# Attention with the value products in groups of four key steps, and the exponentials in a ring of eight

## The reference

```python
qkv = jnp.einsum('bsd,od->bso', x, w_project)          # x is layer-normed, 1 x 2048 x 512
q, k, v = (qkv[0], qkv[1], qkv[2])                     # 16 heads of 32
att = jnp.einsum('bhqd,bhkd->bhqk', q, k) / math.sqrt(HEAD_DIM)
att = jnp.where(causal[None, None, :, :], jnp.float32(-1000000000.0), att)
att = jax.nn.softmax(att, axis=-1)
out = jnp.einsum('bhqk,bhkd->bhqd', att, v)
return jnp.einsum('bsd,od->bso', out, w_out)           # and x + this
```

## Time and profile before

| | |
|---|---|
| median of 3 runs | 3358.98 us (3356.23 to 3374.25) |
| profiled execution: its own time is its span | 3356.4 us |
| TensorE matmuls, busy share of the span | 93% |
| DVE / ACT / POOL | 62% / 47% / 26% |
| attention, pairs 1 to 7 and the tail | about 291 to 820 us of the span |

### The profile page before, as it was taken

One profiled execution on the slowest core, in us unless ns is written; L12 is line 12 of the kernel. 1 busy time (PEld: TensorE's weight loads), 2 busy tenths in 40 slices (PEclk: granted clock), 3 DMA queues, 4 the chain that ended last, 5 costly groups with the idle time before them and its releaser, 6 DMA issues. The chain is left out here.

```text
span 3356.4 us, 62801 instructions
## 1 busy us (share of the span) xinstructions
PE 3138.2 (93%) x15964; PEld 2447.5 (73%) x15965; DVE 2074.8 (62%) x3588; ACT 1589.8 (47%) x2095; POOL 885.0 (26%) x768
## 2 busy tenths in 40 slices
PE   7979999999899899999999968878998999999996
PEld 6745555555577699999999933336777999999995
DVE  4256666663585466666666649988654666666664
ACT  2224444444321256665665656634124665565663
POOL 0011000010011233334343314430122444343432
PEclk9969999999999999999999979989998999999998
DMA  5331111130310367777777540124016777777765
GB/s 175 114 76 40 40 40 39 40 99 4 114 37 23 110 174 167 174 175 167 182 180 173 109 131 0 50 72 159 21 42 173 180 174 178 175 172 175 168 139 111
DMA packets 141339, 383.49 MB, mean 114 GB/s; under 512 B 22112, under 2 KB 22880, under 8 KB 137568
## 3 DMA queue, kind: packets, MB, share of 16 engines
q1 hardware_dynamic: 87456, 252.66, 24.1%
q0 software_dynamic: 52608, 127.69, 20.1%
q10 hardware_dynamic: 1152, 1.57, 0.2%
HBM read 281.42 MB, written 104.63 MB: 115 GB/s over the span
## 5 line engine op out<-in xcount | busy, mean ns | idle before, releaser
L1727 DVE TENSOR_TENSOR first_lo<-first_raw,first_hi x232 | 562.8, 2426 | 118.9 <-ACT first_hi L1670 118.4
L1624 POOL DMA_INDIRECT acc_rows<-g_y,first_ids_out x232 | 377.6, 1628 | 896.3 <-ACT g_y L1681 698.3
L594 DVE TENSOR_REDUCE b_part_max<-b_p_ring 128x1 f32<-128x512 f32 (+3 forms) x640 | 360.1, 606 | 230.9 <-PE b_p_ring L681 143.4
L1670 ACT ACTIVATE first_hi<-first_raw x232 | 469.5, 2024 | 49.9 <-DMA first_raw<-in_expert_weights_dram 30.9
L568 ACT ACTIVATE b_probs<-b_p_cols 128x1024 f32<-128x1024 f32 (+1 forms) x320 | 269.2, 893 | 322.5 <-PE b_p_cols L699 322.5
L1720 DVE TENSOR_TENSOR g_hidden<-g_gate,g_p_up 128x352 f32<-128x352 f32 x232 | 120.9, 521 | 449.2 <-PE g_p_up L1787 444.8
L1785 PE MATMUL g_p_gate<-first_hi,g_rows_hi 128*128 x928 | 321.6, 347 | 6.7 <-DVE first_lo L1727 6.4
L1681 ACT ACTIVATE g_y<-g_p_y,first_rows_in 128x512 f32<-128x512 f32 x232 | 159.4, 687 | 331.0 <-PE g_p_y L1803 331.0
L1786 PE MATMUL g_p_gate<-first_lo,g_rows_hi 128*128 x928 | 302.6, 326 | 0.0
L1787 PE MATMUL g_p_gate<-first_hi,g_rows_lo 128*128 x928 | 301.5, 325 | 0.0
L1786 PE MATMUL g_p_up<-first_lo,g_rows_hi 128*128 x928 | 298.6, 322 | 0.0
(11 more groups left out here) (327 smaller groups left out, 6435.1 us busy)
## 6 DMA issues: line engine op xcount, KB each, us to landing
first_raw<-in_expert_weights_dram SPq DMA_DIRECT2D x248, 544.0 KB
acc_rows<-f_acc SPq DMA_DIRECT2D x34, 256.0 KB, 2.0
qk_hi<-a_hi SPq DMA_DIRECT2D x32, 256.0 KB, 2.6
qk_lo<-a_lo SPq DMA_DIRECT2D x32, 256.0 KB, 2.9
xn_rows<-f_xn SPq DMA_DIRECT2D x8, 1024.0 KB, 10.5
b_q_stack<-qk_hi SPq DMA_DIRECT2D x28, 256.0 KB
b_k_stack<-qk_hi SPq DMA_DIRECT2D x28, 256.0 KB
first_raw<-in_expert_weights_dram SPq DMA_DIRECT2D x2, 2176.0 KB, 9.4
```

Of the source, the lines that this page charges most:

```text
L594: v.tensor_reduce(part_max[:, h, t % BT, c:c + 1], p_ring[:, ring, 0:w], AX.X, ALU.max).then_inc(rows_free, 1)
L1624: pool.indirect_dma_start(out=acc_rows, out_offset=bass.IndirectOffsetOnAxis(ap=ids_out[:, i:i + 1].bitcast(U32), axis=0), in_=y[:, n, :], ...
L1670: act.activation(hi[:, bass.ds(place, PIECE)], raw[:, bass.ds(source, PIECE)], ACT.Copy).then_inc(split_hi_ready, 1)
L1727: v.tensor_tensor(lo[:, bass.ds(place, PIECE)], raw[:, bass.ds(source, PIECE)], hi[:, bass.ds(place, PIECE)].bitcast(F32), ALU.subtract).t ...
```

## The change

`probs` is no longer a buffer of its own with four places but eight places in the memory of `resid`. `LAG` becomes 4, and `products` run only in every second turn of the loop over m (m = 2, 6, 10, ...), four steps at a time: at m the steps m-6 to m-3, at m = 2 the last four of the pair before. The residual rows, which can't be loaded while the exponentials lie there, are loaded in `stage_attn_out`, by a new block on SP.

```diff
-    NPROB, NCOL, NRING = 4, 2, 3
-    LAG, LEAD = 2, 22
+    NPROB, NCOL, NRING = 8, 2, 3
+    LAG, LEAD = 4, 22
...
-        probs = sb("b_probs", [P, NPROB, HPAIR, BW])
+        probs = resid[:].rearrange("p (q h) c -> p q h c", h=HPAIR)
...
                         sp.dma_start(values[:, 0:KD, :], wo).then_inc(wo_loaded, 16)
-                        for b in range(NB):
-                            sp.dma_start(resid[:, place_of(b):place_of(b) + BT, :], rows(x)[:, b * BT:(b + 1) * BT, :]).then_inc(x_loaded, 16)
...
                 sp.wait_ge(wo_loaded, 16)
-                sp.wait_ge(x_loaded, 16 * NB)
...
-                        for before in (m - LAG, m - LAG + 1):
+                        if m % LAG == 0:
+                            continue
+                        for before in range(m - 2 - LAG, m - 2):
                             if before >= 0:
                                 products(n, i, before)
                             elif not is_first(n):
...
+            @block.sync
+            def _(sp):
+                for b in range(NB):
+                    sp.dma_start(resid[:, place_of(b):place_of(b) + BT, :], rows(x)[:, b * BT:(b + 1) * BT, :]).then_inc(x_loaded[b], 16)
...
                     v.wait_ge(product, t + 1)
+                    if t % BT == 0:
+                        v.wait_ge(x_loaded[t // BT], 16)
```

More of the change, by code:

```diff
@@ L421, in stage_attention @@
         first_loaded = [k.sem(f"b_first_loaded{j}") for j in range(NB)]
-        x_loaded, wo_loaded = k.sem("b_x_loaded"), k.sem("b_wo_loaded")
+        wo_loaded = k.sem("b_wo_loaded")
         LOADED = HPAIR * 6 * 16
@@ L772, in _, with stage_attn_out @@
                 turn_out(NPAIR - 1, NB - 1, bank("out", NSTEP))
-def stage_attn_out(k, w, ident, heads, resid):
+def stage_attn_out(k, w, ident, heads, x, resid):
     nc = k.nc
@@ L789, in stage_attn_out @@
         product, added = k.sem("c_product"), k.sem("c_added")
+        x_loaded = [k.sem(f"c_x_loaded{b}") for b in range(NB)]
         with nc.Block() as block:
+            @block.sync
+            def _(sp):
+                for b in range(NB):
+                    sp.dma_start(resid[:, place_of(b):place_of(b) + BT, :], rows(x)[:, b * BT:(b + 1) * BT, :]).then_inc(x_loaded[b], 16)
             @block.scalar
@@ L2275, in attention @@
                 k.end_stage()
-                stage_attn_out(k, values[:, 0:KD, :], ident, heads, resid)
+                stage_attn_out(k, values[:, 0:KD, :], ident, heads, x2, resid)
                 k.end_stage()
```

## The result

| | before | after |
|---|---|---|
| median | 3359.04 us | 3436.43 us (3434.13 to 3448.04, 4 runs) |
| ratio | 1 | 1.0226 (95%: 1.0195 to 1.0257) |
| span of the profiled execution | 3356.4 us | 3432.4 us |
| scores of step 0 of pairs 1, 3, 4 | 291.0, 444.9, 524.4 | 296.6, 474.3, 562.6 |
| first transpose of the stage behind attention | 821.4 | 901.3 |

The change is 77 us slower, inside the forecast range of 3380 to 3442 and 18 us above its middle. All of it lies in attention: the stage behind starts 80 us later, and what follows takes 2531 us against 2535. From one step 0 to the next, pairs 1 to 6 take 86.7 to 89.2 us, 88.1 on average, where the forecast expected 82 to 83 and the kernel before has 77.1.

What follows compares the result with a forecast made beforehand. The prediction took attention to be bound by PE. Its terms summed as 3356.4 - 28 + 52.6 + 9 + 18 + 8 = 3416.0, plus 2.6 against the median of the runs: 3418 us, range 3380 to 3442.

Steps and rivals of the forecast that it cites:

- term 5: Clock after PE's six new stops: half of them drop it, at 1 to 3.4 us each; +8 us, between 0 and 20.
- Term 1: PE in attention: 80 fewer changes between products and the rest, at 0.35 us each; -28 us.
- Term 2: Pairs 0 to 6: eight row units between groups wait for `p_ring` and `p_cols`; +52.6 us, between 19 and 79.
- the walk: Term 2's step-by-step arithmetic through a pair: ten stretches wait 9.7 us, against 2.0 before.
- Term 3: Last pair: third and fourth scores of each four wait for exponentials, 0.81 and 0.46 us; with ring waits +9 us.
- Term 4: Pairs 1 to 6: block 2's shift lands late behind the stack loads, scores(12) wait 3 us; +18 us, between 0 and 28.
- Term 6: Residual loads in the next stage: hidden, at most 3 us late; 0.
- Rival A: Ring waits without the late shift's loss, which gets past the loads or swallows ring waits; clock loss falls too; 3393, chance 0.17.
- Rival B: Only the saved changes count, as queues smooth the bunched units: -28 us stands alone, 3331; chance 0.06.
- rival D: The clock drops in most pairs, 10 us each, and waits are at their upper bound: 3442 and over; chance 0.09.

Runs made afterwards that it cites:

- e1: The changed kernel with the shift of block 2 written and read back ahead of the stack loads in pairs 1 to 6; 3398.4 us, ratio 1.0116.
- e2: e1 with the grouping undone: products two steps at a time in every turn, four steps behind the scores; 3365.3 us, ratio 1.0026.
- e5: e1 with DVE's row maxima taken over at most the first 128 of up to 512 columns; 3344.2 us, ratio 0.9950.
- e6: The kernel before with the shift ahead of the stack loads and row maxima over at most 128 columns; 3340.0 us, ratio 0.9933.
- e3: e1 with the products of the last pair alone two steps at a time in every turn; 3388.5 us, ratio 1.0094.
- e4: The kernel before with the stack loads of pairs 1 to 6 held until two more steps of products are done; 3405.1 us, ratio 1.0131.
- e8: The kernel before with the shift of block 2 ahead of the stack loads; 3359.8 us, ratio 1.0001.
- e7: The change with twelve more matmuls, later written over, in front of scores(12) of pairs 1 to 6; 3424.4 us, ratio 1.0178.
- e9: The change with the old lag and order of products, keeping the ring in the residual rows' memory and later residual loads; 3361.9 us, ratio 1.0003.

## Why the prediction came out right, point by point

The mechanisms that it named are the ones in the traces. The total fell into the range with errors on both sides, and that part is luck. Two of its signs did not come true. PE's idle time grew, from 218 to 259 us over the span, but its busy time did not fall: it went from 3138 to 3174 us, since matmuls at half clock are busy for longer (2.07 us against 0.98 above). And a pair takes 88.1 us and not 82 to 83. Its own terms give more than that, 76.1 - 3.5 + 7.7 + 3 = 83.3, and 84.6 with the clock; the rest is mostly term 5.

- **Term 1, the saved changes (-28).** The price of a change stands: in the cycle of four above, the products take 3.58 us where eight passes at 0.43 are 3.44, and the last two scores 0.67 where 0.46 are theirs, together 0.35 again. The sum was not measured alone, since even with cheap maxima other waits fill the place. With terms 2 and 3 it makes up the price of the grouping, -28 + 52.6 + 9 = 34 us; e1 minus e2 is 33 (30 by the ratios). Both hold some clock: 23.8 us at half clock in e1, 10.2 in e2.
- **Term 2, the ring.** The mechanism is shown by e5 and e6: with DVE cheap, 34 us more come back in the grouped order than in the other. Its sizes stood up by place too. Leaving out drops of the clock, e1 is 5.0 us a pair above the kernel before, where 7.7 - 3.5 = 4.2 were forecast, and 4.0 above e2. The largest rises are at steps 28 to 31 (1.6 us), then 0 to 3, 20 to 23 and 16 to 19 (1.0 to 1.1); three of these were named. (The ten waits of the walk add up to 9.8, not 9.7.) The walk put the ungrouped kernel's own waits for DVE too low (20 us gained in e6).
- **Term 3, the last pair.** Its two waits are in the trace of after to 0.01 us. Net of ten changes the forecast was 9 - 3.5 = 5.5 us; the pair is 8.3 us longer than before, 76.0 against 67.7. e3 is 5.9 below the change, which fits this term; the 2.4 that e3 keeps over the kernel before go with the longer lag.
- **Term 4, the shift (18).** Measured 18.3, six stops. The issue of the loads came at 7.6 us into the pair ("about 7" was forecast), and the shift took 12.5 us instead of 11.2. e4 shows the mechanism without the grouping, e8 that it was hidden before. The forecast read the long landing as siding with the second half of the rule of the Trainium skill, "DMA: Bandwidth & Descriptors", section "Queues, rings and completion order", a semaphore that lands only after all earlier writes. The packets do not bear that out for most of it: for about nine of the 12.5 us the shift's own data had not started. The number was right, and that reason for it was not shown.
- **Term 5, the clock (8): the term that was mis-sized.** "Six times, half of them, 1 to 3.4 us each" should have been all six, 6.8 to 10.2 us at half clock, 2.9 to 4.3 us each: 22.8 us. That alone moves 3418 to 3433. e4 leaves 20 us beside its stops (46 less 26); e1 and e7 gave back less than the full 23 because drops of 3.4 us came up elsewhere. The forecast compared only with a stop of 3.64 us, as if that length were needed. Its other case, the half clock from 445 to 455, stands right behind a stop of 2.04 us in the kernel before:

```profile
444.37 0.76 PE L681 MATMUL b_p_ring<-b_k_stack,b_q_stack 96*128 96x512 f32 x2 [2.04 <-issue]
```

- **Term 6, the residual loads (0).** The first sum of the next stage comes 9.9 us behind its first transpose, 911.23 against 901.33, and is released by PE. e9 confirms it.
- **Left out, a cost:** the longer lag has a price of its own, 3 to 6 us (e2 against e9 and before). Term 2 held a part of it (the 2.8 us at steps 0 to 3).
- **Left out, a gain:** PE of the kernel before stood still for 2.04 and 1.74 us where its loop starts anew (pairs 3 and 5), and the half clock behind the first cost 3.8 us (steps 0 to 3 of pair 3 took 11.4 us, against 7.6 in pairs 1, 2 and 4). In the change sixteen product matmuls run there, and 0.6 us of the two stops are left. These 7 us hid a part of what term 5 was short of.

Rival A, the ring alone, is e1: it came out at 3398 where it was given 3393. But its condition did not occur. Rival B fell to the waits for DVE, and e5 shows that it would not have won with DVE cheap either. Of rival D, given 0.09, the first half came true: the clock dropped in every pair, four times for 10.2 us and twice for 6.8. It came out under its 3442 because the waits were not at their upper bound.

## What to carry to other kernels

An order that gives one engine longer blocks takes cover from all others: before grouping, ask of each block what the others finish behind it, and count how many buffers they would need in the stretch between blocks. An engine that is busy for only 62% of the time can still be the bound within such a stretch. When an edit moves a semaphore's release, follow every queue that waits for it, because a small transfer behind large ones may be the one that has no time to spare. A stop of PE of some 3 us costs about twice its length here, and filling it with throwaway matmuls got back a good part of the second half. When an edit removes a drop of the clock, count the drops afterwards: here new ones came up elsewhere and took back part of the gain.

## What the runs showed of the hardware that was not expected

- Stops of PE of 2.6 to 5 us each came with half clock for 6.8 to 10.2 us, beginning between 2 us before and 1 us behind the end of the stop, twelve of twelve in the change and e4. Each drop cost 2.9 to 4.3 us beside the stop in the change (22.8 us over six).
- Shorter stops could do it or not. In the kernel before the one of 2.04 us was followed by 10.2 us at half clock and the one of 1.74 us by none; in e8 both are 1.93 us, and half clock, 6.8 us, follows the first alone.
- Even without a long stop the grouped kernel loses clock. In e1 a window in pair 1, behind several short ring waits:

```profile
336.00:340.70 4.70, 3.82 (x20) 2.45 (x19) 4.05 (x10) 2.86 (x5) 1.58 (x4) 1.00 0.01 2
340.70:344.10 3.40, 3.36 (x10) 1.40 (x12) 0.47 (x2) 0.00 (x0) 0.00 (x0) 0.50 0.02 5
```

The granted clock is 1.00 in the first window and 0.50 in the second, with no stop as long as those of the change between them. The forecast had no term for it. Its price can be read off: steps 20 to 23 take 10.4 to 10.7 us in pairs 1 to 5 of e1, which all have such a drop there, and 9.05 in pair 6, which has none. That is 1.4 to 1.7 us for 3.4 us at half clock, and about 11 us over the seven drops of e1 from pair 1 on.
